# Indices and attention kept on chip, features three quads ahead, and the sort's turns copied by VectorE in a two-layer graph network

## The chip, the cores and the metric

The kernel runs on one core of one Trainium2 chip. The metric is the device time of one launch in microseconds (us), median of three runs. The engines are named as in the profile: PE is TensorE, DVE VectorE, ACT ScalarE, POOL GpSimd, SP SyncE; SPq and ACTq are the DMA queues that SP and ACT feed.

## What is computed

A network of two layers on a graph of 6250 nodes with 64 features each and 206,250 edges. The edges are the pairs of 100,000 drawn ones, both ways, and one loop for each node, sorted by dst. All is float32.

```
h = relu(layernorm(x));  row, col = src, dst
# layer 0: four heads
e   = concat(h[row], h[col])
a   = pos[col] * exp(lrelu(gate_w2 @ lrelu(gate_w1 @ e)))
x   = x + mean over heads of segment_sum(a / segment_sum(a)[row] * lrelu(msg_w2 @ lrelu(msg_w1 @ e)), row)
h = relu(layernorm(x))
# layer 1: feat = edge_attr (64 numbers an edge), attn = edge_weight
m   = (h[src] * sigmoid(feat @ prob_w.T) + (feat @ review_w.T) * sigmoid(feat @ score_w.T) * attn) * cj[src]
x   = x + segment_sum(m, dst) * ci
```

## The kernel before

The edges are padded to 404 blocks of 512 (128 partitions, T = 4 tiles); 403 of them (NBW) hold edges. Four blocks are a quad, 101 quads (NQ) in all. The kernel uses that dst is sorted: a block's edges end in a narrow window of nodes, whose rows are read with one plain transfer, while the rows of src are gathered by index. The program has these stages.

Setup (0 to about 320 us). Loads, the layernorm on DVE, then the loop over the 49 node tiles that writes the table of window rows: PE turns and projects a tile (L1999, L2008, L2009, L2019), ACT copies it (L1020, L1027, L1034), SP stores it. SP issues the setup's loads in the order of the program text; `loaded` counts 17 of them, from the first weights to the four of gate_w2 (L543), and ACT's L1037 waits for all.

Layer 0 (320 to 3640 us). Per block PE runs twelve matmuls of 512 columns (L1870, L1871) and many smaller ones; POOL gathers the rows of src from split_table (L774) with the indices in src_pairs, which SP loads two blocks at a time (load_index), after it has waited until the gathers that read the old ones are done. Sums are scattered to DRAM by POOL.

The node update between the layers takes to about 3704 us and ends in src_table, which holds a node's features and cj.

Layer 1 (3704 to 6366 us). Each engine has a program of its own in the order of the blocks b (m = b mod 4 is the place in the quad), tied to the others by semaphores.
- SP, load1_windows: at m = 0 it waits for `terms1_step` 16·(quad−1), which says that quad−2 is done and its buffers are free, then loads the quad's indices (src_quads, L592), features (512 KB, L594) and attention (attn_quads, L596), each in two buffers; then it waits for `out_ready` quad−1 and loads the x and ci windows (L624, L625).
- POOL, gather1_windows (L827): at m = 0 it waits for those three loads. In every block it waits for `terms1_step` 4·(b−3), that is until DVE is through with block b−4, whose gather buffer it fills (four buffers, ends1_windows), and issues four indirect gathers.
- DVE: two products of the features with the gates' weights (L1740), two reductions to dots (L1746); at m = 1 finish_rows for quad−2, which waits for PE's projection and writes the rows of the output (L1755); at m = 2 match_carry (L1761); the one-hot matrix (L1772); a part of the check; then feat_gate (L1777, waits for ACT's sigmoid), the terms (L1779, waits for the gather), L1782 and L1785. The last four step `terms1_step`, so L1785 is the end of a block on DVE.
- ACT: the sigmoid (L1132), copy_window (L1156) and send_rows (L1173, the store of the output rows) at m = 2, copy_turned (L1162, waits for PE's turn of the window) at the last m.
- PE: eight matmuls of a block (L2107) into ps_beta, at the quad's end the carry (L2112), the turn of the window (L2124), the projections (L2130, L2131).

The check runs beside layer 1: it sorts keys of the edges and compares them with the mirrored list; its result decides at the end whether the form with windows stands or a general form is run. sort_plan lays it on blocks from 10 to MIRROR = 380. HALVES are steps on DVE (L1644, L1647, up to 128x1024 elements), ROUNDS are turns: PE transposes four 128x128 pieces of a run into one PSUM bank (turn_bank, ps_hidden[2]), ACT copies the bank to the other list (L1116, or L1118 with a sign), two rounds in each of 28 blocks, so 56, and four more for the mirrored list (L1125). One bank serves all, so each turn waits for the copy before it. The columns and dot weights that DVE reads in every block (columns_ps, dots_w_ps) lie in another bank, ps_T.

## Time and profile before

| | us |
|---|---|
| median of 3 runs | 6369.76 |
| fastest, slowest | 6354.51, 6380.25 |
| the profiled execution, its own time | 6382.29 |
| its span | 6380.7 |
| PE, DVE, ACT, POOL busy | 4448.9, 4638.8, 2628.9, 3558.8 |
| setup, layer 0, update, layer 1 | 0 to 320, 320 to 3640, 3640 to 3704, 3704 to 6366 |

The span runs from the first to the last instruction of the profiled execution. An engine's busy time is the sum of its instructions without their waits. No engine is busy for more than 73% of the span, and the shares are means over stages with different limits, so the argument is made stage by stage. "<-issue" is idle time in which the engine waited for nothing that the profile shows; "<-remote" is a wait whose releaser the profile doesn't name.

### The profile page before, as it was taken

What the parts mean: (1) busy time and instruction counts of PE and PEld (TensorE: products, weight loads), DVE (VectorE), ACT (ScalarE), POOL (GpSimd) and SP (SyncE); (2) the same over time, 40 slices, a digit from 0 to 9 for tenths busy, and PEclk for the clock granted to TensorE, in tenths of its full rate; (3) what the DMA queues carried; (4) which work ended last, traced back from release to release, by engine and by line L of the source; (5) the groups of instructions that cost most, each with busy time, mean ns of one, the idle gap of its engine ahead of it and who ended that gap; (6) DMA issues with size and microseconds to landing.
All of it is one profiled execution on the core that took longest, in us unless ns stands there. A gap on an engine that the chain in (4) does not pass through costs nothing.

```text
span 6380.7 us, 112465 instructions
## 1 busy us (share of the span) xinstructions
PE 4448.9 (70%) x25026; PEld 2772.9 (43%) x25026; DVE 4638.8 (73%) x10169; ACT 2628.9 (41%) x6414; POOL 3558.8 (56%) x3640
## 2 busy tenths in 40 slices
PE   5799999999999999999999723333344443344443
PEld 4455555555555555555555323333333333333333
DVE  3488888888888888888888766666666666666664
ACT  3666667666666666666666510000000000000000
POOL 0255555555555555555555355656656556666664
PEclk8999999999999999999999855555555555555555
DMA  7533333333333333333333322222222222222222
GB/s 195 184 75 74 75 76 74 75 75 75 74 75 73 77 73 74 75 75 75 75 75 75 87 81 42 44 43 44 44 42 43 43 43 43 47 44 43 44 44 39
DMA packets 484894, 436.01 MB, mean 68 GB/s; under 512 B 294336, under 2 KB 366240, under 8 KB 483744
## 3 DMA queue, kind: packets, MB, share of 16 engines
q0 software_dynamic: 122512, 173.81, 15.7%
q1 hardware_dynamic: 334416, 247.54, 14.7%
q10 hardware_dynamic: 27840, 13.23, 1.1%
q8 instruction: 48, 0.79, 0.1%
q14 instruction: 78, 0.64, 0.0%
HBM read 363.28 MB, written 70.96 MB: 68 GB/s over the span
## 4 chain that ended last, share of the span: by engine, by line
PE 39%; issue 25%; DVE 10%; POOL 6%; SPq 6%; DMA 5%; ACT 4%; another core or an unknown queue 4%; DVEq 1%; ACTq 0%; POOLq 0%
PE ps_beta L1922 12%; PE ps_hidden L1870 8%; PE ps_hidden L1871 7%; POOL work L827 4%; DVE work L1358 3%; PE ps_sum L1941 3%; POOL ends L827 3%; PE ps_beta L1930 3%; PE ps_alpha L1904 1%; DMA attn_quads<-in_edge_weight 1%; SPq L592 1%; DMA ends<-src_table,src_quads 1%; PE ps_alpha L1913 1%; ACT beta_scaled L969 1%
## 5 line engine op out<-in xcount | busy, mean ns | idle before, releaser
L774 POOL DMA_INDIRECT ends<-split_table,src_pairs x1612 | 1578.0, 979 | 1615.7 <-issue 1459.6
L827 POOL DMA_INDIRECT work<-src_table,src_quads x808 | 806.8, 998 | 856.4 <-DMA attn_quads<-in_edge_weight 361.8
L1870 PE MATMUL ps_hidden<-ends_parts,w_high 128*128 128x512 f32 x2418 | 1097.4, 454 | 159.2 <-ACT ends_hot L964 60.0
L1358 DVE TENSOR_TENSOR work<-work,ps_hidden 128x512 f32<-128x512 f32 x1612 | 1101.0, 683 | 54.7 <-ACT work L911 43.5
L2107 PE MATMUL ps_beta<-work,equal 128*128 128x128 f32 x1616 | 411.4, 435 | 904.8 <-DVE work L1785 540.2
L911 ACT ACTIVATE work<-ps_hidden 128x512 f32<-128x512 f32 x1612 | 947.2, 600 | 219.3 <-PE ps_hidden L1871 179.6
L1871 PE MATMUL ps_hidden<-ends_hot,window 128*128 128x512 f32 x2418 | 954.5, 395 | 4.1 <-issue 3.8
L827 POOL DMA_INDIRECT ends<-src_table,src_quads x804 | 802.7, 998 | 257.9 <-issue 244.1
L1363 DVE TENSOR_TENSOR beta<-beta_scaled,ps_beta 128x512 f32<-128x512 f32 x806 | 551.4, 684 | 418.1 <-ACT beta_scaled L969 346.5
L1132 ACT ACTIVATE ps_alpha<-dots 128x8 f32<-128x8 f32 x403 | 72.4, 180 | 1876.9 <-DVE dots L1746 1336.8
L2107 PE MATMUL ps_beta<-work,dst_rows_sb 128*128 128x128 f32 x1608 | 411.4, 437 | 609.6 <-DVE work L1785 430.1
L1922 PE MATMUL ps_beta<-work,msg_w_sb 128*64 128x512 f32 x3224 | 827.6, 611 | 4.6 <-issue 0.9
L1870 PEld LDWEIGHTS ps_hidden<-ends_parts,w_high 128*128 128x128 f32 x2418 | 453.7, 188 | 793.3 <-DVE work L1358 436.0
L969 ACT ACTIVATE beta_scaled<-ps_beta 128x512 f32<-128x512 f32 x806 | 484.9, 602 | 701.8 <-PE ps_beta L1922 663.3
L2107 PEld LDWEIGHTS ps_beta<-work,equal 128*128 128x128 f32 x1616 | 354.5, 323 | 951.7 <-DVE work L1785 563.9
L2107 PEld LDWEIGHTS ps_beta<-work,dst_rows_sb 128*128 128x128 f32 x1608 | 355.2, 325 | 679.3 <-DVE work L1785 482.2
L1358 DVE TENSOR_TENSOR work<-scaled,ps_hidden 128x512 f32<-128x512 f32 x806 | 545.9, 677 | 25.7 <-ACT scaled L911 13.7
L911 ACT ACTIVATE scaled<-ps_hidden 128x512 f32<-128x512 f32 x806 | 486.0, 603 | 149.0 <-PE ps_hidden L1871 144.9
L1930 PE MATMUL ps_beta<-ident,beta 128*128 128x128 f32 x3224 | 506.1, 279 | 0.8 <-DVE beta L1363 0.7
L1871 PEld LDWEIGHTS ps_hidden<-ends_hot,window 128*128 128x128 f32 x2418 | 457.7, 189 | 44.3 <-issue 4.3
L1930 PEld LDWEIGHTS ps_beta<-ident,beta 128*128 128x128 f32 x3224 | 357.2, 141 | 167.6 <-issue 146.6
L788 POOL DMA_DIRECT2D sums<-key_rows x403 | 373.6, 927 | 75.1 <-issue 46.8
(202 smaller groups left out, 6703.2 us busy)
## 6 DMA issues: line engine op xcount, KB each, us to landing
window<-window_table SPq DMA_DIRECT2D x403, 192.5 KB
parts<-in_edge_attr SPq DMA_DIRECT2D x101, 512.0 KB
dst_rows_sb<-in_dst_rows SPq DMA_DIRECT2D x403, 128.0 KB
ends<-split_table,src_pairs POOLq DMA_INDIRECT x1612
window_table<-parts SPq DMA_DIRECT2D x49, 386.0 KB
sums<-key_rows POOLq DMA_DIRECT2D x403, 32.6 KB
work<-src_table,src_quads POOLq DMA_INDIRECT x808
ends<-src_table,src_quads POOLq DMA_INDIRECT x804
```

Of the source, the lines that this page charges most:

```text
L774: pool.indirect_dma_start(out=ends[m][:, t, :], out_offset=None, in_=split_table, in_offset=bass.IndirectOffsetOnAxis(ap=src_pairs[m // 2] ...
L788: pool.dma_start(sums0[0][bass.ds(first, WIN0), :], quad_sum[m * WIN0:(m + 1) * WIN0, :], accum_op=ALU.add).then_inc(quad_added, 16)
L827: pool.indirect_dma_start(out=ends1_windows[m][:, t, :], out_offset=None, in_=src_table, in_offset=bass.IndirectOffsetOnAxis(ap=src_quads[ ...
L911: nc.scalar.activation(scaled[k % NL][:, :], ps_hidden[k % NL][:, :], ACT.Copy, scale=SLOPE).then_inc(scaled_ready, 1)
L969: nc.scalar.activation(beta_scaled[:, a * B:(a + 1) * B], ps_beta[a][:, :], ACT.Copy, scale=SLOPE).then_inc(beta_scaled_ready, 1)
L1358: nc.vector.tensor_tensor(hidden[k][:, :], scaled[k % NL][:, :], ps_hidden[k % NL][:, :], ALU.max).then_inc(hidden_ready, 1)
L1363: nc.vector.tensor_tensor(beta_T[a], beta_scaled[:, a * B:(a + 1) * B], ps_beta[a][:, :], ALU.max).then_inc(beta_ready, 1)
L1870: nc.tensor.matmul(o, w1_high[:, k * P:(k + 1) * P], ends_parts[j][:, :], start=True, stop=False)
L1871: nc.tensor.matmul(o, window[j][:, k * P:(k + 1) * P], ends_hot[j][:, :], start=False, stop=True).then_inc(hidden_done, 1)
L1922: last = nc.tensor.matmul(ps_beta[a][i * D:(i + 1) * D, :], msg_w2_sb[:, 2 * a + i, :], hidden[2 + 2 * a + i][:, :], start=True, stop=True)
L1930: last = nc.tensor.transpose(ps_beta[a][:, t * P:(t + 1) * P], beta_T[a][:, t * P:(t + 1) * P], ident[:, :])
L2107: last = nc.tensor.matmul(ps_beta[odd][0:WIN, 0:W1], hot_four[m][:, t, :], terms1_windows[m][:, t, :], start=(m == 0 and t == 0), stop=(m ...
```

## The change

1. The indices (src) and attention of all blocks are kept on chip. In setup SP loads eight pieces of up to 128 block rows (128x512, 1.65 MB in all), four of each, ahead of the loads of gate_w2; DVE casts the indices to float at tile 11 of the loop over node tiles, PE turns each piece with four transposes (between tiles 14 and 33), DVE copies them to src_all and attn_all. POOL waits for the indices before its first gather, PE for both before layer 0. load_index, src_pairs, src_quads and attn_quads go, and with them POOL's waits on loads.
2. The features of layer 1 lie in four buffers instead of two. SP asks for quad+3 once quad−1 is done.
3. send_rows is issued by SP, between the load of the features and that of the x window, no longer by ACT.
4. PE turns the sort's pieces a block earlier and into two banks in turn (ps_hidden[2], ps_T), DVE copies them (move_rounds), in place of ACT. The mirrored list is added two pieces a block. columns_ps and dots_w_ps move from ps_T to ps_sum.
5. POOL's programs of both layers are written out block by block, where they were loops of hardware.

```diff
@@ SP, setup and layer 0
-            def load_index(b, a):
-                sp.dma_start(src_pairs[a][:, :].rearrange("p (b t) -> p b t", t=T),
-                             src[bass.ds(b, 2)].rearrange("b p t -> p b t")).then_inc(index_in[a], 16)
-            for a in range(2):
-                load_index(2 * a, a)
+            for k in range(4):
+                n = min(P, NB - k * P)
+                sp.dma_start(rows_sb[k][0:n, :].bitcast(I32),
+                             src_rows[k * P:k * P + n].rearrange("b t p -> b (t p)")).then_inc(rows_in[0], 16)
+            for k in range(4):
+                n = min(P, NB - k * P)
+                sp.dma_start(rows_sb[4 + k][0:n, :],
+                             edge_weight[k * P:k * P + n].rearrange("b p t -> b (p t)")).then_inc(rows_in[1], 16)
...
-                if m % 2 == 1 and not (isinstance(b, int) and b >= NB - 4):
-                    for n in (m - 1, m):
-                        sp.wait_ge(gathered0[n], 64 * (quad + 1))
-                        settle(sp)
-                    load_index(b + 3, m // 2)
@@ SP, layer 1
-            def load1_quad(quad, odd):
...
+            def load_feat(quad):
+                k = quad % 4
+                sp.dma_start(feat_quads[k].rearrange("p b t d -> p b (t d)"),
+                             edge_attr[bass.ds(4 * quad, 4)].rearrange("b p t d -> p b (t d)")).then_inc(feat_in[k], 16)
...
-            def load1_windows(b, quad, half, m, odd):
-                if m == 0 and not first_quads(quad):
-                    sp.wait_ge(terms1_step, 16 * (quad - 1))
-                    settle(sp)
-                    load1_quad(quad, odd)
-                    sp.wait_ge(out_ready, quad - 1)
-                    settle(sp)
-                if m == 0:
-                    load_x_window(quad, odd)
...
-            quads(sp, load1_windows)
+            sp.wait_ge(part_free, NCH)
+            load_feat(3)
+            for quad in range(NQ):
+                if quad >= 1 and quad + 3 < NQ:
+                    sp.wait_ge(terms1_step, 16 * quad)
+                    load_feat(quad + 3)
+                if quad >= 2:
+                    send_rows(quad - 2)
+                load_x_window(quad)
@@ POOL
-                pool.wait_ge(index_in[m // 2], 16 * (quad + 1))
...
-                        in_offset=bass.IndirectOffsetOnAxis(ap=src_pairs[m // 2][:, m % 2 * T + t:m % 2 * T + t + 1],
+                        in_offset=bass.IndirectOffsetOnAxis(ap=src_all[:, b * T + t:b * T + t + 1],
...
+            pool.wait_ge(src_ready, 4)
...
-            fours(pool, edges0_windows)
+            for b in range(NBW):
+                edges0_windows(b, b // 4, b % 4)
...
-                if m == 0:
-                    pool.wait_ge(edge_in1w[odd], 48 * (half + 1))
                 if not first_four(b):
                     pool.wait_ge(terms1_step, 4 * (b - 3))
...
-                        in_offset=bass.IndirectOffsetOnAxis(ap=src_quads[odd][:, m, t:t + 1], axis=0)).then_inc(gathered1w[m], 16)
+                        in_offset=bass.IndirectOffsetOnAxis(ap=src_all[:, b * T + t:b * T + t + 1], axis=0)).then_inc(gathered1w[m], 16)
...
-            quads(pool, edges1_windows)
+            every_block(edges1_windows)
@@ ACT, layer 1
-                if b in ROUNDS:
-                    move_rounds(*ROUNDS[b])
-                if b - MIRROR in (0, 1):
-                    mirror_rounds(2 * (b - MIRROR))
-                if m == 2 and not (isinstance(quad, int) and quad < 2):
-                    send_rows(quad - 2, odd)
@@ DVE
+            def cast_rows():
+
+                dve.wait_ge(rows_in[0], 64)
+                for k in range(4):
+                    n = min(P, NB - k * P)
+                    nc.vector.tensor_copy(rows_sb[k][0:n, :], rows_sb[k][0:n, :].bitcast(I32)).then_inc(rows_cast, 1)
+
+            def keep_rows(a, k):
+
+                dve.wait_ge(rows_turned, 4 * a + k + 1)
+                n = min(P, NB - k * P)
+                kept = (src_all, attn_all)[a].rearrange("p (b t) -> p t b", t=T)[:, :, k * P:k * P + n]
+                nc.vector.tensor_copy(kept, row_banks[k % 2][:, :].rearrange("p (t b) -> p t b", b=P)[:, :, 0:n]).then_inc(src_ready, 1)
...
+            def move_rounds(n, first, of, turned_by):
+
+                for i in range(first, first + 2):
+                    dve.wait_ge(sort_turned, 4 * n + i + 1)
+                    if turned_by is None:
+                        nc.vector.tensor_copy(runs[1 - of][:, i * B:(i + 1) * B], turn_banks[i % 2][:, :]).then_inc(sort_moved, 1)
+                    else:
+                        nc.vector.tensor_scalar(runs[1 - of][:, i * B:(i + 1) * B], turn_banks[i % 2][:, :],
+                                                signs[:, turned_by:turned_by + 1], None, ALU.mult).then_inc(sort_moved, 1)
...
                 if m == 0:
-                    dve.wait_ge(edge_in1w[odd], 48 * (half + 1))
+                    dve.wait_ge(feat_in[quad % 4], 16 * (quad // 4 + 1))
@@ PE
+            def turn_rows(a, k):
...
+                for c in range(T):
+                    rows = (rows_sb[k][0:n, c * P:(c + 1) * P] if a == 0 else
+                            rows_sb[4 + k][0:n, :].rearrange("b (p t) -> b t p", t=T)[:, c, :])
+                    last = nc.tensor.transpose(row_banks[k % 2][:, c * P:c * P + n], rows, ident[0:n, 0:n])
+                last.then_inc(rows_turned, 1)
...
+            pe.wait_ge(src_ready, 8)
...
-                wait(pe, sort_moved, 4 * n + i)
+                wait(pe, sort_moved, 4 * n + i - 1)
                 for c in range(4):
-                    last = nc.tensor.transpose(turn_bank[:, c * P:(c + 1) * P],
+                    last = nc.tensor.transpose(turn_banks[i % 2][:, c * P:(c + 1) * P],
                                                runs[of][:, (4 * i + c) * P:(4 * i + c + 1) * P], ident[:, :])
```

## Rows read from the trace of the kernel before

**Rows 1.** Windows by stage: start:end, length, busy of each engine, PEclk, DMA, GB/s.
```profile
36.00:235.00 199.00, 133.56 (x684) 98.52 (x682) 22.65 (x78) 91.19 (x245) 11.52 (x12) 0.87 0.87 252
320.00:3640.00 3320.00, 3166.62 (x19672) 1728.50 (x19670) 2808.14 (x5510) 2275.68 (x5209) 1895.74 (x1961) 1.00 0.35 74
3704.00:6366.00 2662.00, 1059.92 (x4166) 895.80 (x4166) 1660.45 (x4330) 160.49 (x661) 1609.48 (x1612) 0.51 0.23 45
```

**Rows 2.** Lines of POOL in layer 1: busy, mean ns of one, idle before and releasers.
```profile
L827 POOL DMA_INDIRECT work<-src_table,src_quads x808 | 806.8, 998 | 856.4 <-DMA attn_quads<-in_edge_weight 361.8 <-issue 241.3 <-DVE work L1785 110.2
L827 POOL DMA_INDIRECT ends<-src_table,src_quads x804 | 802.7, 998 | 257.9 <-issue 244.1 <-DVE work L1785 13.5 <-DVE ps_sum L1782 0.3
```

**Rows 3.** Windows of three runs of gathers with the pause behind each.
```profile
3704.00:3767.00 63.00, 13.23 (x51) 11.46 (x52) 24.89 (x65) 1.36 (x7) 37.93 (x41) 0.50 0.34 97
4907.50:4962.00 54.50, 19.44 (x75) 16.68 (x76) 31.67 (x81) 1.98 (x11) 33.04 (x32) 0.50 0.22 42
5409.70:5436.30 26.60, 13.44 (x52) 11.52 (x53) 17.93 (x46) 1.27 (x6) 16.01 (x16) 0.50 0.23 43
```

**Rows 4.** Timeline of the second run's end: start, length, instruction, idle before it.
```profile
4935.03 0.69 PE L2131 MATMUL ps_hidden<-window_sum,ident 128*128 128x64 f32 x2
...
4949.05 0.94 POOL L827 DMA_INDIRECT ends<-src_table,src_quads  x1 [0.30 <-issue]
4953.21 0.28 DVE L1755 SCALAR_TENSOR_TENSOR parts<-ps_hidden,ci_windows,parts 128x64 f32<-128x64 f32 x1 [14.36 <-remote]
...
4955.86 0.42 DVE L1785 TENSOR_TENSOR work<-parts,ps_sum 128x256 f32<-128x256 f32 x1
4955.89 0.38 SPq L592 DMA_DIRECT2D src_quads<-in_src  x1
...
4962.15 0.94 POOL L827 DMA_INDIRECT work<-src_table,src_quads  x1 [12.15 <-DMA attn_quads<-in_edge_weight]
```

**Rows 5.** Waits named "remote": us in total, times, longest.
```profile
ACT parts L1162 <- remote: 238.3, 57, 19.8
...
DVE parts L1755 <- remote: 158.6, 18, 14.5
```

**Rows 6.** Setup: timeline of SPq, ACT, DVE and PE, and PE's line L1930.
```profile
8.75 1.51 SPq L535 DMA_DIRECT2D src_pairs<-in_src  x2
...
22.14 0.83 ACT L1037 ACTIVATE near_parts<-w_near 128x768 fp32r<-128x768 f32 x1
...
33.22 0.20 DVE L1247 COPY table_sb<-pos_sb 128x49 f32<-128x49 f32 x1
...
151.72 0.19 PEld L2008 LDWEIGHTS ps_beta<-near_parts,h_T 128*128 128x128 f32 x1 [0.65 <-ACT h_T L1020]
...
L1930 PE MATMUL ps_beta<-ident,beta 128*128 128x128 f32 x3224 | 506.1, 279 | 0.8 <-DVE beta L1363 0.7
```

**Rows 7.** Lines: POOL's gathers in layer 0.
```profile
L774 POOL DMA_INDIRECT ends<-split_table,src_pairs x1612 | 1578.0, 979 | 1615.7 <-issue 1459.6
```

**Rows 8.** Lines of DVE in layer 1: the mirrored list's addition out of a bank.
```profile
L1694 DVE TENSOR_TENSOR x_sb<-ps_hidden,table_sb 128x512 f32<-128x512 f32 x4 | 2.8, 692 | 18.6 <-PE ps_hidden L2069 9.7 <-remote 7.8 <-issue 1.1
```

**Rows 9.** Timeline: gathers beside DVE's L1740 and beside L1647.
```profile
5004.89 0.74 DVE L1740 TENSOR_TENSOR work<-parts,ps_T 128x256 f32<-128x256 f32 x2
...
5005.28 0.94 POOL L827 DMA_INDIRECT ends<-src_table,src_quads  x1 [0.30 <-issue]
...
5014.41 1.22 DVE L1647 TENSOR_TENSOR centered<-table_sb 128x1024 f32<-128x1024 f32 x1
5014.59 1.86 POOL L827 DMA_INDIRECT work<-src_table,src_quads  x1 [0.31 <-issue]
```

**Rows 10.** Timeline: the end of the first run of gathers.
```profile
3752.82 0.94 POOL L827 DMA_INDIRECT work<-src_table,src_quads  x1 [0.30 <-issue]
...
3759.62 0.35 DVE L1761 TENSOR_SCALAR parts<-ps_T,carry_at 128x128 f32<-128x128 f32 x1 [7.33 <-remote]
...
3766.95 0.94 POOL L827 DMA_INDIRECT ends<-src_table,src_quads  x1 [13.19 <-DVE work L1785]
```

More of the change, by code:

```diff
@@ L133, in gnn @@
         ones = sb("ones", [1, P])
-        w1_near = sb("w1_near", [P, HID])
+        first_rows = sb("first_rows", [P, NB * T])
+        w1_near, w1_far = [first_rows[:, a * HID:(a + 1) * HID] for a in range(2)]
+        attn_all = first_rows[:, :]
         columns = sb("columns", [P, WIN])
@@ L328, in gnn @@
         window_copied = sem("window_copied")
-        edge_in1w = [sem(f"edge_in1w{j}") for j in range(2)]
+        feat_in = [sem(f"feat_in{k}") for k in range(4)]
+        rows_in = [sem(f"rows_in{a}") for a in range(2)]
+        rows_cast = sem("rows_cast")
+        rows_turned = sem("rows_turned")
+        src_ready = sem("src_ready")
         gathered1w = [sem(f"gathered1w{m}") for m in range(4)]
@@ L352, in gnn @@
         begun_again = sem("begun_again")
-        index_in = [sem(f"index_in{a}") for a in range(2)]
         gathered0 = [sem(f"gathered0_{m}") for m in range(4)]
@@ L477, in sort_plan @@
         def sort_plan():
-            halves, rounds, of, steps, moved, turn, b = {}, {}, 0, 1, 0, 0, SORT_FROM
+            halves, rounds, moves, of, steps, moved, turn, b = {}, {}, {}, 0, 1, 0, 0, SORT_FROM
             def kept(run):
@@ L494, in sort_plan @@
                     for r in range(2):
-                        rounds[b + r] = (turn, 2 * r, of, None if inward or k == SORT_BITS else k - RUN_BITS, steps)
+                        rounds[b - 1 + r] = (turn, 2 * r, of, steps)
+                        moves[b + r] = (turn, 2 * r, of, None if inward or k == SORT_BITS else k - RUN_BITS)
                     of, turn, moved, b = 1 - of, turn + 1, 4 * turn + 4, b + 2
@@ L499, in sort_plan @@
                         of, steps, b = two_halves(1 << i, run, inward and i == k - RUN_BITS - 1, RUN)
-            return halves, rounds, of, steps, turn, b
-        HALVES, ROUNDS, SORTED, SORT_STEPS, TURNS, MIRROR = sort_plan()
-        SETTLE = MIRROR + 6
+            return halves, rounds, moves, of, steps, turn, b
+        HALVES, ROUNDS, MOVES, SORTED, SORT_STEPS, TURNS, MIRROR = sort_plan()
+        SETTLE = MIRROR + 5
         assert SETTLE + 9 < NBW
@@ L603, in _ @@
             for quad in range(2):
-                load1_quad(quad, quad)
+                load_feat(quad)
             sp.wait_ge(sums0_landed, 1)
@@ L626, in load_x_window, with send_rows @@
                              ).then_inc(x_window_in[odd], 16)
+            def send_rows(quad):
+                first = window_start(sp, 4 * quad)
+                sp.wait_ge(out_ready, quad + 1)
+                if quad == 0:
+                    sp.wait_ge(out_set, 16)
+                else:
+                    sp.wait_ge(rows_out, 16 * quad)
+                settle(sp)
+                sp.dma_start(out[bass.ds(first, WIN), :], out_rows[quad % 2]).then_inc(rows_out, 16)
             sp.wait_ge(x_summed, 2 * NCH)
@@ L1162, in copy_turned @@
                 nc.scalar.activation(sum_T, sum_turned, ACT.Copy).then_inc(sum_T_ready, 1)
-            def send_rows(quad, odd):
-                first = window_start(act, 4 * quad)
-                act.wait_ge(out_ready, quad + 1)
-                if isinstance(quad, int) and quad == 0:
-                    act.wait_ge(out_set, 16)
-                else:
-                    act.wait_ge(rows_out, 16 * quad)
-                settle(act)
-                act.dma_start(out[bass.ds(first, WIN), :], out_rows[odd]).then_inc(rows_out, 16)
             copy_constants()
             every_block(edges1_windows)
-            send_rows(NQ - 2, (NQ - 2) % 2)
             copy_window(NQ - 1, (NQ - 1) % 2)
             copy_turned(NQ - 1)
-            send_rows(NQ - 1, (NQ - 1) % 2)
             fit = fits(act)
@@ L1517, in _ @@
                     signs_of_lanes()
+                elif t == 11:
+                    cast_rows()
+                elif 18 <= t < 38 and t % 6 < 2:
+                    keep_rows((t - 18) // 12, 2 * ((t - 18) // 6 % 2) + t % 6)
             dve.wait_ge(fits_step, 9)
@@ L1713, in settle_part @@
                     dve.wait_ge(reach_turned, 1)
-                    nc.vector.tensor_reduce(out=reach[0:1, 7:8], in_=turn_bank[0:1, 0:P], axis=AX.X,
+                    nc.vector.tensor_reduce(out=reach[0:1, 7:8], in_=turn_banks[0][0:1, 0:P], axis=AX.X,
                                             op=ALU.max).then_inc(mirror_step, 1)
```

127 lines of the change are left out of this document (67 added, 60 removed).

## The prediction

> **What bounds the kernel now.** I read the windows by stage first, then the lines and waits of POOL in the second layer, then the windows of single runs of gathers, then the timeline inside one of them, then the waits put down to "remote".
>
> By stage [rows 1]: the first layer's main loop (320 to 3640 us) has PE busy 3166.62 of 3320 us. PE is its bound, and at 95% busy it leaves nothing to an edit that touches only loads. The second layer (3704 to 6366) lasts 2662 us and no engine fills it: POOL 1609, DVE 1660, PE 1060, ACT 160. It handles 403 blocks of 512 edges, 2662 / 403 = 6.606 us each, and issues 1612 indirect gathers, four to a block.
>
> POOL is the engine to follow there [rows 2]. One gather takes 0.998 us and is followed by some 0.30 us of issue time (244.1 / 804): 1.30 us, so 5.19 us a block and 2093 us for all. The other 569 us of the stage are pauses of POOL. The rows put 361.8 us of them down to the DMA of the quad's attention and indices and 110.2 to DVE's L1785, which is the wait for a free gather buffer. DVE needs 1660 / 403 = 4.12 us a block, less than POOL's 5.19. So POOL would be the bound were it not stopped.
>
> The stops have a period [rows 3]. From 4907.5 to 4962.0 POOL does 32 gathers (8 blocks) and then pauses: 54.5 us, 6.81 a block. From 5409.7 to 5436.3 it does 16 gathers in 26.6 us, 6.65 a block. The first run, from 3704 to 3767, has 40 gathers (its 41st row is the next run's) in 63 us. The view says "DMA", but the timeline [rows 4] shows what lies behind the DMA. PE's last matmul of the quad, L2131, ends at 4935.72. DVE wants its result (L1755) and starts only at 4953.21, after 14.36 us "remote", with no unfinished matmul in front of it. All that time POOL issues gathers, to 4949.99. DVE is released 3.2 us after POOL's last gather and finishes its block (L1785 ends 4956.28); SP then issues the held index load (L592 at 4955.89), and POOL goes on at 4962.15, 12.15 us after it stopped. So the loop is a circle: while POOL issues gathers without a pause, PE's completion signals reach DVE and ACT late; DVE stops; POOL runs on until it has no work left; the signal lands; the load and then POOL start again. The waits named "remote" [rows 5] are this: ACT L1162 238.3 us, DVE L1755 158.6 us (18 times, longest 14.5). Only what comes after DVE's release is the DMA.
>
> **The change part by part.**
> Setup. Eight row loads are added to SP's queue ahead of the loads of gate_w2, two index loads are taken out. At the 0.76 us of one of those two (1.51 / 2) [rows 6] the queue grows by 6 × 0.76 = 4.5 us. Everything that ACT's L1037 waits for has landed by 22.14 now; with 4.5 us and the 1.65 MB of the rows at the 252 GB/s of [rows 1] (6.5 us) it lands by 33.1, and DVE wants L1037's result after L1247, at 33.4: hidden, at worst 0.5 us late. The 32 transposes (8 × 4) cost 0.28 us each by L1930, 9.0 us, in a loop of 49 steps, each of which has PE wait for ACT's h_T (its weight load at 151.72 after 0.65 us). Bounds 0 (they fit in the 65 us that PE is idle from 36 to 235) and +15 (9.0 plus a semaphore turn of 0.7, an estimate from that 0.65, for each of eight). I take +5. DVE's 4 casts and 8 copies lie in 176 us of idle DVE.
> First layer. 202 small index loads, SP's waits on finished gathers and POOL's waits on the loads go. POOL's gathers of this stage show 1615.7 us of idle time before them [rows 7], and the bound is PE: 0, bounds −10 and +5 (POOL's loop is unrolled, whose instruction fetch this trace does not show).
> Second layer, indices and features. POOL no longer waits for a load, so SP's late index load can't stop it, and features are there two quads earlier. What is late next is the free buffer. DVE stopped in block b (L1755 is in the second block of a quad) lets POOL gather up to block b+3, where now it stops with the quad, at b+2: a run of 32 gathers becomes one of 36. Its length: the run that began at 4907.5 ended at 4949.99, 42.5 us for 32, 1.33 each, so 36 × 1.33 = 47.8 us. Its pause: 3.2 us from the last gather to the late signal, 3.1 us until DVE ends that block (4953.21 to 4956.28), 0.7 us to POOL's start (estimate, a semaphore turn as above): 7.0 us instead of 12.15. The cycle is 54.8 us for 9 blocks, 6.09 a block. Were the stop to come 25 us after the start of a run (in [rows 4] it is 31), 11 us of run-ahead and 7.0 us of pause give 43.3 us for 29 gathers, 5.97 a block. The first run of all, whose indices were there from the start, took 6.30. I take 6.05, the middle of the first two moved a little towards the third: 403 × 6.05 = 2438 us, −224. The waits at L1785 (110.2 us now) become the rule and are no term of their own. Bounds of the part: −569 (no pauses) and +70 (the slower rival).
> Sort turns. 60 copies of 128x512 out of a bank move from ACT to DVE. DVE's own operation on such a bank, L1694, takes 0.692 us [rows 8]: 60 × 0.69 = 41 us, 0.10 a block, against a slack of 5.19 − 4.12 = 1.07. POOL's pace hides it; with DVE on the path it would be +41: bounds 0 and +41. PE turns a block earlier, so DVE seldom waits for a timely turn. A late one now stops DVE itself in 30 blocks, where before it stopped ACT and DVE behind it: 0, bounds −40 and +40.
> What DVE's copies do to POOL. The gather beside DVE's L1647, which has two inputs in SBUF, lasts 1.86 us; the one beside L1740, whose second input is a bank, 0.94 [rows 9]. The copies have one input, a bank, and so cost POOL nothing; if they acted as L1647 it would be 60 × 0.92 = +55 us. The Trainium skill ("SBUF — State Buffer", section "Who interferes with whom") says that a DVE instruction with at most one SBUF input outside the 2-port modes does not contend with GpSimd and that one with two contends with its reads. The trace agrees on both, and by the rule, too, the term is 0.
> Output rows. send_rows leaves ACT's queue for SP's. The wait it makes (the rows of quad−2, finished in the second block of the quad) stood in SP's queue already, ahead of load_x_window, and the features are asked for before it. Behind it is only the x window, which is read two quads later. 0.
> Sum on the profiled execution (6382.29 us, span 6380.7): −224 + 5 = −219, 6163. That execution lies 12.5 us above the median of the three timed runs (6369.76), so against the median I say 6150.
>
> **The rivals.**
> A: the late signals come from something that goes with the index waits, and POOL keeps its pace. The second layer takes 403 × 5.19 = 2093 us: 6382 − 569 + 5 − 12 = 5806. For it: DVE has 1.07 us a block to spare, and four buffers. Against it: in [rows 4] DVE waits for PE, not for an index, and the first run stopped as well, after 40 gathers. The Trainium skill, in the same section, says "PE and ACT never wait on anyone"; by that rule nothing that POOL does could hold PE's results back, and this rival alone would be left. The trace disagrees: 14.36 us between a finished matmul and its reader. Half-way cases (rarer or shorter stops) give 5880 to 6040.
> B, slower: the release takes longer the longer POOL has run, because more signals stand in line. After 32 gathers it came 3.2 us behind the last one. In the first run [rows 10] the last of 40 gathers ended at 3753.76, DVE was released at 3759.62, 5.9 us later, and POOL's pause was 13.19 us with no DMA in it. With 36 gathers in 47.8 us the cycle is even with now at 9 × 6.606 − 47.8 = 11.7 us of pause; beyond it the change loses. With 13.2: 61.0 / 9 = 6.78 us a block, 2732, +70: 6382 + 70 + 5 − 12 = 6445. For it: that pause. Against it: that run was longer, and its gathers took 1.25 us each, so that even with it a block took 6.30.
> C, no change: DVE's stops follow the number of signals it needs from PE, not POOL's runs, and what a pause loses in length it gains in number: 6340 to 6400. For it: runs of 16 and of 32 gathers come to 6.65 and 6.81 a block, near each other. Against it: in both, some 6 us from DVE's release to POOL's first gather are the load's, and go.
>
> **How the numbers follow.** The forecast has 0.50, with a range of its own of 6040 to 6260 (5.8 to 6.33 us a block); A 0.20; between A and the forecast 0.10; C 0.10; B 0.10. The range is 5800 to 6320: it takes in A and the bounds of the unknown costs above the forecast (+15, +41, +55 and +40, not all at once) and leaves out B and C. Faster by over 0.5%: 0.50 + 0.20 + 0.10 = 0.80; within 0.5% (about what can be told from no change here): 0.10; slower: 0.10.
>
> **What would show it.** POOL's waits on a load of indices are gone, its pauses are released by DVE's last operation of a block and last about 7 us, after runs of some 36 gathers (12 us or more: B; runs of hundreds: A). "Remote" waits stay at DVE's finish_rows and ACT's copy_turned. The second layer lasts about 2440 us, the first layer's loop stays within 10 us, setup grows by 5. DVE's copies out of the banks take 0.6 to 0.7 us, with gathers of 0.94 beside them. The prediction is wrong if the signals come in time without a pause of POOL, or if the stops move into the first layer.

## The result and the profile after

| | us |
|---|---|
| before, median of 4 runs | 6369.69 (6354.51 to 6380.25) |
| changed, median of 4 runs | 6123.82 (6118.99 to 6131.07) |
| ratio, 95% interval | 0.9603 (0.9581 to 0.9626) |
| profiled executions, before and changed | 6382.29 and 6118.99 |
| forecast, range | 6150, 5800 to 6320 |

The changed kernel is 4.0% faster. Between the two profiled executions the time by stages, taken from the first product of layer 0 to the first one of its last block and from the first to the last gather of layer 1, is:

| stage | before | changed | difference | forecast |
|---|---|---|---|---|
| setup, to the first product | 235.9 | 230.8 | −5.1 | +5 |
| layer 0, to the last block's product | 3388.9 | 3315.4 | −73.5 | 0 |
| update, to the first gather of layer 1 | 79.2 | 80.4 | +1.2 | 0 |
| layer 1, to the last gather's start | 2660.1 | 2469.2 | −190.9 | −224 |
| the end | 16.6 | 20.5 | +3.9 | 0 |

The windows of the changed kernel, in the columns of [rows 1]: setup's loop, layer 0, layer 1.

```profile
36.00:230.80 194.80, 132.13 (x716) 98.73 (x715) 30.66 (x91) 90.61 (x245) 11.56 (x12) 0.91 0.87 258
230.80:3546.20 3315.40, 3217.47 (x20102) 1774.82 (x20103) 2871.58 (x5630) 2341.52 (x5333) 1932.97 (x1998) 1.00 0.34 76
3626.60:6096.70 2470.10, 1049.57 (x4154) 890.52 (x4155) 1671.29 (x4377) 114.59 (x598) 1618.44 (x1612) 0.52 0.23 47
```

Layer 1 takes 2470 / 403 = 6.13 us a block; 6.05 was forecast, 6.61 it was. ACT's busy time fell from 160 to 115 us, and the pace is still set by no engine's busy time: POOL has 1618 of 2470 us. Its lines, which answer to [rows 2], and its waits (total, times, longest):

```profile
L839 POOL DMA_INDIRECT ends<-src_table,parts x804 | 813.0, 1011 | 313.4 <-issue 240.6 <-DVE work L1800 72.8
L839 POOL DMA_INDIRECT work<-src_table,parts x808 | 805.5, 997 | 601.0 <-DVE work L1800 308.4 <-issue 229.9 <-DMA src_table<-table_sb 62.8
```
```profile
POOL work L839 <- DVE work L1800: 308.4, 124, 7.5
POOL ends L839 <- DVE work L1800: 72.8, 44, 10.4
```

The DMA of the indices is gone from them. L1800 is the old L1785, the end of DVE's block: POOL now pauses only for a free buffer, 381 us in all, where it lost 361.8 to the load and some 124 to that. The waits for PE's signals did not go, they grew; the rows answer to [rows 5], L1150 being the old L1162 and L1770 the old L1755:

```profile
ACT parts L1150 <- remote: 432.5, 39, 19.7
DVE parts L1770 <- remote: 379.1, 55, 15.3
...
ACT ps_alpha L1126 <- remote: 56.4, 7, 12.4
...
DVE ps_sum L1797 <- remote: 52.2, 15, 5.2
```

The last two rows are not about PE: L1126 is ACT's sigmoid, which waits for DVE's dots, and L1797 (the old L1782) waits only for DVE's own operations in front of it. So what is late is not PE's signals alone.

Counted in both traces (gaps of more than 2 us between gathers), POOL's pauses went from 87 of 6.66 us on the mean to 77 of 4.75 us, 579 to 366 us. A timeline of the changed kernel, to be held against [rows 4], shows one stop with its parts:

```profile
4771.97 0.42 PE L2160 MATMUL ps_hidden<-ident,window_sum 128*64 128x128 f32 x1
...
4783.59 0.95 POOL L839 DMA_INDIRECT ends<-src_table,parts  x1 [0.31 <-issue]
4786.96 0.27 ACT L1150 ACTIVATE parts<-ps_hidden 64x128 f32<-64x128 f32 x1 [15.38 <-remote]
...
4788.06 0.42 DVE L1800 TENSOR_TENSOR work<-parts,ps_sum 128x256 f32<-128x256 f32 x1
...
4789.26 0.95 POOL L839 DMA_INDIRECT work<-src_table,parts  x1 [4.72 <-DVE work L1800]
```

PE turned the window by 4772.39; ACT, which waits for it, starts at 4786.96, 2.4 us after POOL's last gather of this run of 32 ended (4784.54). ACT's sigmoid stands behind that copy, DVE behind the sigmoid, and POOL behind DVE's L1800: 2.4 + 1.5 to the end of L1800 + 0.8 = 4.7 us. It is the circle of the forecast without its load.

But not every late signal waits for such a pause. Layer 1 has 130 waits named remote of over 2 us, 109 of them for PE (the others for DVE). Of the 109, 64 end in a pause of POOL (a gap of over 1 us) and 45 in the midst of its gathers; in the kernel before these were 71 and 19 of 91. One of DVE's for PE ended 45 us after POOL's last pause:

```profile
4662.69 0.95 POOL L839 DMA_INDIRECT work<-src_table,parts  x1 [0.31 <-issue]
4663.68 0.28 DVE L1770 SCALAR_TENSOR_TENSOR parts<-ps_hidden,ci_windows,parts 128x64 f32<-128x64 f32 x1 [10.79 <-remote]
...
4663.94 0.95 POOL L839 DMA_INDIRECT work<-src_table,parts  x1 [0.30 <-issue]
```

### The profile page after: what moved, and what is told of

It reads as the page before. It is cut to its first block, busy times and chain, and to the rows that moved or that the text cites. A ratio compares the mean times of both kernels' runs of the same rounds, so it can differ in the third digit from the quotient of the medians.

```text
span 6116.3 us, 108132 instructions
## 1 busy us (share of the span) xinstructions
PE 4418.4 (72%) x25058; PEld 2776.0 (45%) x25058; DVE 4662.3 (76%) x10241; ACT 2592.6 (42%) x6354; POOL 3568.6 (58%) x3639
## 4 chain that ended last, share of the span: by engine, by line
PE 38%; DVE 32%; issue 12%; another core or an unknown queue 12%; ACT 3%; DMA 1%; DVEq 1%; ACTq 0%; POOL 0%; SPq 0%; POOLq 0%
PE ps_beta L1937 11%; PE ps_hidden L1885 8%; PE ps_hidden L1886 6%; DVE dots L1761 4%; DVE work L1333 4%; PE ps_beta L1945 3%; PE ps_sum L1956 3%; DVE table_sb L1640 3%; DVE work L1755 3%; DVE centered L1640 3%; DVE work L1794 2%; DVE work L1800 2%; PE ps_alpha L1919 2%; DVE equal L1787 2%
## 5 line engine op out<-in xcount | busy, mean ns | idle before, releaser
L786 POOL DMA_INDIRECT ends<-split_table,parts x1612 | 1581.0, 981 | 1532.9 <-issue 1399.2
L839 POOL DMA_INDIRECT work<-src_table,parts x808 | 805.5, 997 | 601.0 <-DVE work L1800 308.4
L839 POOL DMA_INDIRECT ends<-src_table,parts x804 | 813.0, 1011 | 313.4 <-issue 240.6
L1126 ACT ACTIVATE ps_alpha<-dots 128x8 f32<-128x8 f32 x403 | 72.0, 179 | 1841.8 <-DVE dots L1761 1156.8
```

The source lines that it names most:

```text
L786: pool.indirect_dma_start(out=ends[m][:, t, :], out_offset=None, in_=split_table, in_offset=bass.IndirectOffsetOnAxis(ap=src_all[:, b * T ...
L839: pool.indirect_dma_start(out=ends1_windows[m][:, t, :], out_offset=None, in_=src_table, in_offset=bass.IndirectOffsetOnAxis(ap=src_all[:, ...
```

## The experiments

Each number of a stage below is read as in the table above, and each ratio is to the kernel before of the same session, with its 95% interval. The runs fell into four sessions, and the kernel before, run in each beside the others, took 6370.87, 5618.80, 6307.43 and 5621.26 us in them. That is itself the main finding, and it comes with the second session. (The expectations call the sessions chips; what the runs show is only that the same kernel took another time.)

**POOL's loops written out, nothing else** (before 6370.87).

```diff
-            fours(pool, edges0_windows)
+            for b in range(NBW):
+                edges0_windows(b, b // 4, b % 4)
...
-            quads(pool, edges1_windows)
+            every_block(edges1_windows)
```

> The kernel before, with POOL's programs of both layers written out block by block; nothing else. Layer 0 became 73 us shorter with the change (3389 us from the first product to the last before, 3315 after), where I had counted nothing. Theory U (POOL's loop of hardware delays its gathers or what waits for them): this run shows layer 0 at about 3320 us and the whole some 70 us shorter than before. Theory L (the small index loads on SP's queue, their packets and SP's waits on gathers cost it): layer 0 stays at 3389 within 8 us. In layer 1 both expect 2660 us within 20, since the loads and POOL's wait for them are still there.

Measured: 6379.76 us, ratio 1.001 (0.9991 to 1.0029). Layer 0 3381.8, layer 1 2672.1 us. Of the 73.5 us of layer 0 the loops have at most the 7 that it is shorter here, and nothing of layer 1's gain; theory U falls.

**Layer 0's small index loads put back** (before 6370.87).

```diff
+                if m % 2 == 1 and not (isinstance(b, int) and b >= NB - 4):
+                    for n in (m - 1, m):
+                        sp.wait_ge(gathered0[n], 64 * (quad + 1))
+                        settle(sp)
+                    sp.wait_ge(index_in[m // 2], 16 * quad)
+                    settle(sp)
+                    load_index(b + 3, m // 2)
```

> The changed kernel with layer 0's 202 small index loads put back on SP's queue, with SP's waits for the gathers before them, into tiles that nobody reads and with nobody waiting for them. Theory L expects layer 0 back at about 3389 us (+73) and the whole near 6197. Theory U expects no change: layer 0 at 3315 within 8, the whole 6124 within 15. A part of it would say that POOL's wait for the load, which this run lacks, had the rest. Layer 1 stays at 2469 within 20 in both.

Measured: 6209.89 us, ratio 0.9728 (0.9702 to 0.9754), 86 us above the changed kernel. Layer 0 3393.2 us (+77.8), layer 1 2478.3. Theory L holds, and without an engine that waits for these loads (SP alone asks that the one of a quad earlier has landed): 200 loads (the first two are not repeated) of 256 pieces of 16 bytes, with SP's waits, cost layer 0 its 78 us. PE, the bound, idles 143 us of layer 0 here, 98 in the changed kernel and 148 in the one before; the other 33 of the 78 us are longer busy time of the same matmuls, which no row explains. In the idle time the wait for ACT's copy ends_hot moves (before, changed, this run):

```profile
PE ps_hidden L1870 <- ACT ends_hot L964: 60.0, 94, 1.0
```
```profile
PE ps_hidden L1885 <- ACT ends_hot L976: 9.2, 40, 0.6
```
```profile
PE ps_hidden L1898 <- ACT ends_hot L989: 44.2, 81, 0.9
```

ACT, in its turn, is held at the copies of PE's product; its line over the same 1600 us (1000 to 2600) of the changed kernel and of this one:

```profile
L923 ACT ACTIVATE work<-ps_hidden 128x512 f32<-128x512 f32 x778 | 461.3, 601 | 61.0 <-PE ps_hidden L1886 41.0 <-issue 10.5
```
```profile
L936 ACT ACTIVATE work<-ps_hidden 128x512 f32<-128x512 f32 x759 | 446.7, 600 | 84.4 <-PE ps_hidden L1899 66.8 <-issue 11.9
```

There are four such copies a block: 194.5 blocks in the first, 189.75 in the second. The copies themselves are the same (0.60 us); ACT waits 26 us longer for PE. In all of layer 0 ACT, idle, began such a copy over 1 us after PE's matmul had ended 35 times in the changed kernel, 78 times here and 89 times in the kernel before; so lateness of PE's signals is here too, in small pieces.

**Features as late as before, POOL waits for them** (before 6370.87).

```diff
-                if quad >= 1 and quad + 3 < NQ:
-                    sp.wait_ge(terms1_step, 16 * quad)
-                    load_feat(quad + 3)
+                if quad >= 4:
+                    sp.wait_ge(terms1_step, 16 * (quad - 1))
+                    load_feat(quad)
...
+                if m == 0:
+                    pool.wait_ge(feat_in[quad % 4], 16 * (quad // 4 + 1))
```

> The changed kernel with the features asked for as late as before (quad q once quad q-2 is done) and POOL waiting for them at each quad's first block, as it did for the indices. My forecast's account (the circle of late signals, DVE's stop, and a load that POOL waits for) expects layer 1 to go back from 2469 to about 2640 us (+150 to +190) with POOL's pauses released by a DMA, 5 to 12 us long, and the whole near 6290. Rival: the gain of layer 1 came from somewhere else (the 292 small packets a quad of indices and attention that are gone, code written out, copies on DVE), then layer 1 stays within 30 us of 2469.

Measured: 6332.90 us, ratio 0.9937 (0.9911 to 0.9963), 209 us above the changed kernel; layer 1 2687.8 us (+218.6), layer 0 3310.2. POOL's wait for a load costs what the forecast's account says and more: 29 us more than the upper end of the expectation, with 59 pauses of 10.2 us on the mean. The rival falls. One pause in the timeline of this kernel, with SP's load in it (L596) and POOL 4.7 us behind it; the 10.88 us are 3.7 to the late signal, 2.6 to the load and 4.7 of the load, though the row names an operation of DVE:

```profile
4627.57 0.94 POOL L841 DMA_INDIRECT ends<-src_table,parts  x1 [0.30 <-issue]
4632.17 0.28 DVE L1772 SCALAR_TENSOR_TENSOR parts<-ps_hidden,ci_windows,parts 128x64 f32<-128x64 f32 x1 [2.92 <-remote]
...
4634.73 0.42 SPq L596 DMA_DIRECT2D parts<-in_edge_attr  x1
4639.39 0.94 POOL L841 DMA_INDIRECT work<-src_table,parts  x1 [10.88 <-DVE ps_sum L1799]
```

**finish_rows two blocks later** (before 6370.87).

```diff
-                if m == 1 and not (isinstance(quad, int) and quad < 2):
-                    finish_rows(quad - 2, half - 1, odd)
...
+                if m == last_m(quad) and quad >= 2:
+                    finish_rows(quad - 2, half - 1, odd)
```

> The changed kernel with finish_rows (DVE's wait for PE's projection) moved from the second block of a quad to its last, after the one-hot matrix. Late signals have DVE stop there 55 times for 379 us in the changed kernel, the longest 15.3 us. If DVE stops because it asks for PE's result only about a block and a half after PE was due, two more blocks (12 us) take most of these stops away: DVE's waits there fall below 100 us, the cycle lengthens and layer 1 goes from 2469 towards 2300 us, by 60 to 170 us. Rival: the lateness is held by POOL's run of gathers, not by the time that has passed, so the signal comes only when POOL pauses; then another wait for PE (the window's copy or the one-hot's buffers, four blocks back) stops DVE or ACT a block or two later, POOL's runs become longer by as much as DVE's stop comes later, and layer 1 changes by less than 60 us.

Measured: 6082.40 us, ratio 0.9534 (0.9513 to 0.9554); layer 1 2434.0 us (−35), with 62 pauses instead of 77, of 4.91 us each. It beats both kernels, 41 us under the changed one. But the rival's account is what happened: DVE no longer waits at finish_rows, and DVE and ACT wait elsewhere instead, for PE (L1144, L1150, L1785) and for DVE's own signals (L1126, L1797), and POOL's runs are longer (median 24 gathers for 20). The rival's premise, that a signal comes only when POOL pauses, fits 56 of this run's 91 waits for PE of over 2 us; 35 end in the midst of gathers.

```profile
ACT parts L1150 <- remote: 599.6, 41, 26.0
ACT ps_alpha L1126 <- remote: 118.8, 14, 12.4
DVE ps_sum L1797 <- remote: 118.4, 28, 6.3
ACT window_sum L1144 <- remote: 81.7, 19, 9.5
DVE equal L1785 <- remote: 75.7, 12, 15.1
```

**Three gathers of four left out** (before 5618.80).

```diff
-                for t in range(T):
+                for t in range(1):
...
-                dve.wait_ge(gathered1w[m], 64 * (quad + 1))
+                dve.wait_ge(gathered1w[m], 16 * (quad + 1))
```

> The changed kernel with one indirect gather a block in layer 1 instead of four: three quarters of the rows of src are left out of it, all else is the same. If PE's completion signals are late because POOL issues gathers without a pause, they are timely here: the waits called remote (812 us at ACT's L1150 and DVE's L1770 in the changed kernel) all but go, below 60 us, and layer 1 runs at DVE's own pace, 4.15 us a block and a few tenths for the waits between engines: 1700 to 1900 us. Rival: PE's signals are late for a reason of PE's or of DVE's (its fp32 matmuls, the chain of window, turn and projection): then the remote waits stay above 300 us and layer 1 above 2000 us.

Measured: 5212.18 us, one run; layer 1 1685.8 us, 4.18 a block, and no wait named remote. Both numbers are as the theory expected, but they can't decide it: beside it, with before at 5618.80, the kernels with all gathers have no remote waits either. What it shows is DVE's pace, 4.18 us a block.

**POOL paced by PE's signals**, twice (before 5618.80 and 5621.26).

```diff
                     pool.wait_ge(terms1_step, 4 * (b - 3))
+                    pool.wait_ge(summed1_done, b - 3)
```

> The changed kernel with one more wait of POOL in layer 1: before the gathers of block b it waits until PE's signal of block b-4 is there. POOL then stops of itself as soon as a signal is about a block late, where now it runs on until DVE's stop has used up the four buffers. The late-signals theory (the signals land 2 to 3 us after a gather, if no other follows) expects more and shorter pauses of POOL, about 3 us each after 12 to 16 gathers, DVE's and ACT's remote waits cut to less than half of 812 us, and layer 1 between 2350 and 2470 us (16 gathers in 20.8 us and 3 us of pause are 5.95 us a block, 2398 us). Rival: the pause costs as much as it saves; the sum of pauses is set by how many signals have to land, and layer 1 stays at 2469 within 30, or grows when POOL waits for PE at every block (to 2600).

> The changed kernel with one more wait of POOL in layer 1: before the gathers of block b until PE's signal of block b-4 is there. On a chip where PE's signals come late the theory (they land 2 to 3 us after a gather if no other follows) expects more and shorter pauses of POOL, DVE's and ACT's remote waits less than half of the changed kernel's, and layer 1 shorter than its 2469 us by 20 to 100. Rival: the sum of the pauses is set by the signals that have to land; layer 1 within 30 us of 2469, or up to 2600 when POOL waits for PE at every block. On a chip where they come in time it repeats 5641 in all, with no wait of POOL for PE over 1 us.

Measured: 5641.38 us, ratio 1.0037 (1.0026 to 1.0049), and 5642.59 us, ratio 1.0040 (1.0026 to 1.0054). Layer 1 2125.2 and 2119.4 us, layer 0 3196.1 and 3195.9. Neither expectation was tested, since no signal was late for the new wait to catch; the idea stays open. The second expectation's last sentence held.

**Features late, POOL waits for no load**, twice (before 5618.80 and 6307.43). The first edit of the run with POOL's wait, without its second.

> The changed kernel with the features asked for as late as before (quad q once quad q-2 is done), but with POOL waiting for no load; only DVE waits for the features. With POOL's wait layer 1 took 2688 us, without both it takes 2469. If POOL's wait for the load is what closes the circle, layer 1 stays within 40 us of 2469 here. If the features' early start is what counts (DVE waits for them at a quad's start, then runs late), layer 1 comes to 2600 or more, with DVE's L1755 waiting for the features. I give the first two in three: after a pause POOL goes on at once.

> The changed kernel with the features asked for as late as before, POOL waiting for no load. On a chip where PE's signals come late: if POOL's wait for the load closes the circle, layer 1 stays within 40 us of 2469, where with POOL's wait it took 2688; if the features' early start counts, it comes to 2600 or more, with DVE's L1755 waiting for the features. On a chip where they come in time it repeats 2094 us of layer 1, 5612 in all.

Measured, with before at 5618.80: 5612.44 us, ratio 0.9987 (0.9977 to 0.9996), layer 1 2094.0. With before at 6307.43: 6065.77 us, ratio 0.9625 (0.9603 to 0.9648), layer 1 2437.1, beside 2436.7 of the changed kernel beside it. So the wait of POOL for a load is what closes the circle; that the features are asked for three quads ahead brings nothing. (The run with POOL's wait, 2687.8 us, is of the first session; the 250 us between it and this one are far more than the 32 us between the sessions' changed kernels.)

**Index loads of whole rows**, twice (before 5618.80 and 5621.26).

```diff
-                sp.dma_start(src_pairs[a][:, :].rearrange("p (b t) -> p b t", t=T),
-                             src[bass.ds(b, 2)].rearrange("b p t -> p b t")).then_inc(index_in[a], 16)
+                sp.dma_start(src_pairs[:, :],
+                             src_rows[bass.ds(b, 2)].rearrange("b t p -> (b t) p")).then_inc(index_in[a], 16)
...
-                    sp.wait_ge(index_in[m // 2], 16 * quad)
+                    sp.wait_ge(index_in[1 - m // 2], 16 * (quad + m // 2))
```

The edit is against the run with the small loads. All loads go to one tile, so SP here waits for the load just before, not for that of a quad earlier.

> The changed kernel with the 202 index loads of layer 0 and SP's waits before them, as in the run that took layer 0 from 3315 to 3393 us, but each load reads the same 4 KB as eight whole rows of 512 bytes instead of 256 pieces of 16 bytes. If the small packets do the harm (they hold up what carries PE's signals to ACT and DVE), layer 0 is back at 3315 within 10. If it is SP's waits (the next window's loads issued late behind them) or the load as such, layer 0 stays near 3393.

> The changed kernel with the 202 index loads of layer 0 and SP's waits before them, each load reading the same 4 KB as eight whole rows of 512 bytes instead of 256 pieces of 16 bytes. With the small pieces layer 0 went from 3315 to 3393 us on a chip where PE's signals come late. On such a chip: if the small packets do the harm, layer 0 is within 12 us of the changed kernel's, and the ratio to the kernel before is that of the changed kernel, 0.96; if SP's waits or the load as such do it, layer 0 is 60 us or more longer and the ratio 0.975. On a chip where they come in time it says nothing: layer 0 3196 us, 5643 in all.

Measured: 5642.66 us, ratio 1.0038 (1.0025 to 1.0050), and 5642.77 us, ratio 1.0044 (1.0027 to 1.0060); layer 0 3196.1 and 3196.2 us. As for the packets, this says nothing, for the same reason. But layer 1 of this kernel is that of the changed kernel, and its windows (layers 0 and 1; the run beside 5621.26) show what that one would do where PE's signals are in time:

```profile
225.00:3421.20 3196.20, 3146.54 (x20102) 1789.93 (x20103) 2873.51 (x5630) 2332.94 (x5333) 1936.96 (x1998) 1.00 0.36 79
3500.40:5627.00 2126.60, 1062.67 (x4166) 899.89 (x4166) 1697.52 (x4390) 118.31 (x601) 1635.63 (x1612) 0.51 0.26 55
```

The engines' busy times are those of the changed kernel above within 4%, and so is the granted clock (1.00 and 0.51). POOL issues its 1612 gathers of layer 1 without one gap above 0.32 us. The timeline of a quad's end, to be held against [rows 4], with L2182, L1785 and L1815 for the old L2131, L1755 and L1785:

```profile
4752.58 0.69 PE L2182 MATMUL ps_hidden<-window_sum,ident 128*128 128x64 f32 x2
...
4755.62 0.94 POOL L854 DMA_INDIRECT work<-src_table,parts  x1 [0.30 <-DVE work L1815]
...
4756.60 0.28 DVE L1785 SCALAR_TENSOR_TENSOR parts<-ps_hidden,ci_windows,parts 128x64 f32<-128x64 f32 x1
...
4756.87 0.94 POOL L854 DMA_INDIRECT work<-src_table,parts  x1 [0.30 <-issue]
```

DVE takes PE's result in its turn, without a wait, in the midst of gathers. In layer 0 ACT's copies into work, over 1000 to 2600 us, have 201.5 blocks and hardly a wait for PE; none of them in all of layer 0, idle before, began more than 0.12 us after PE's matmul:

```profile
L938 ACT ACTIVATE work<-ps_hidden 128x512 f32<-128x512 f32 x806 | 481.0, 604 | 25.9 <-issue 8.6 <-PE ps_hidden L1901 4.0
```

The line's other copies (into scaled) wait longer for PE than before, 125 us against 57 in the changed kernel, since ACT comes to them early. What counts is the idle time of PE, the bound: 50 us in all of layer 0, against 98.

**The changed kernel again** (before 6307.43).

> The changed kernel once more, to be read beside the kernel before on the same chip. The last four runs were on a chip on which the kernel before takes 5619 us, not 6370, and no wait for PE is named remote there: POOL issues all 1612 gathers of layer 1 without one pause, 2095 to 2126 us. On such a chip the change has nothing to gain: layer 1 at 2120 us and layer 0 at 3196 as in the two variants that share them, the whole at 5610 to 5645, within 0.5% of the kernel before. On a chip like the first one (before 6370) it repeats 6124 within 15 us. The rival, that the chip is only faster all round, expects the change to keep its 4% on either chip.

Measured: 6066.44 us, ratio 0.9630 (0.9601 to 0.9658): layer 0 3288.7, layer 1 2436.7 us, remote waits at L1150 483 and at L1770 323 us. A session that the expectation doesn't name, 57 us quicker than 6124, with the gain kept (3.7%). Whether it is lost where signals are in time was not run for the changed kernel itself. The two variants nearest to it, the one paced by PE, whose added wait shows nothing above 0.32 us, and the one with whole-row loads, say that it is: 0.4% slower than the kernel before; the one with the features late is 0.1% faster.

## Why the prediction was right, and where it was not

The time was 26 us under the forecast, 6124 for 6150. One half of the forecast's mechanism is shown: PE's signals stay late, the load drops out of the circle, the free buffer takes its place (the waits at L1800; 219 us come back with POOL's wait). The other half, that the signals are late because POOL issues gathers without a pause, and land when it stops, is not. It fits 64 of the 109 waits for PE of over 2 us; 45 end in the midst of gathers, DVE's own signals are late too (L1797), and in the quicker sessions POOL never pauses and no signal is late. So POOL's run of gathers can't be the whole cause, and what it has to do with it stays open. That the total came so near is luck in part: layer 1 gave 33 us less than forecast, layer 0 gave 73.5 that weren't in the sum. By its own steps:

- Setup, +5: it was −5.1. The transposes and copies lie under the loop's waits; POOL's first gather is 50 us later (134.9 for 84.9), which nothing waits for. The lower bound was the better value; the 5 us themselves are hardly beyond what kernels with one setup differ by where before takes 6370 (230.2 to 232.9 us to the first product with the new one, 234.0 and 235.9 with the old).
- Layer 0, 0 with bounds −10 and +5: it was −73.5. This is the step that failed. I read "PE 95% busy" as "nothing to gain from loads". But the 148 us in which PE idled (98 now, 50 where signals are in time) held waits for ACT's copies, which in turn began late after PE's own matmuls, and with the loads and SP's waits back both grew again: +77.8 us in all, 45 of them idle time of PE and 33 its longer busy time.
- Layer 1, −224: it was −190.9, 6.13 us a block for 6.05. The sum is near and its terms are not: runs of 36 gathers with pauses of 7.0 us were forecast, the median run has 20 (16 with the gaps over 1 us) and the mean pause 4.75 us. The signal that lands in a pause is as often for ACT, at copy_turned (26 of the 77), as for DVE at finish_rows (25), where it was 47 and 12 of 87; for ACT's only 1.5 us of DVE's block, not 3.1, are left after it. Both terms are too large, so that their quotient is nearly right, which is luck: 7.0 / 9 = 0.78 us of pause a block forecast, 366 / 403 = 0.91 measured. The forecast's second cycle has a slip besides: its 29 gathers in 36 us are 1.25 us each, where the first cycle takes 1.33; with 1.33 they are 27, the cycle is 6.4 us a block in place of 5.97, and the middle of the two 6.2 in place of 6.05. The measured 6.13 lies between.
- Copies on DVE, 0: right. They take 0.68 us (L1688) and 0.74 with a sign (L1690), and the 42 gathers that overlap one of the 56 take 0.946 us on the mean, 0.948 at most, as the rows and the rule of the Trainium skill ("SBUF — State Buffer", "Who interferes with whom") had it. The timeline shows two. All of POOL's gathers of layer 1 are stretched by 96 us in all, as against 89 before (what each takes above 0.945 us, added up).

```profile
4524.50 0.94 POOL L839 DMA_INDIRECT work<-src_table,parts  x1 [0.30 <-issue]
4524.56 0.68 DVE L1688 COPY table_sb<-ps_hidden 128x512 f32<-128x512 f32 x1
4525.15 0.68 DVE L1688 COPY table_sb<-ps_T 128x512 f32<-128x512 f32 x1
...
4525.75 0.95 POOL L839 DMA_INDIRECT work<-src_table,parts  x1 [0.30 <-issue]
```

- Output rows, 0: nothing in the trace speaks against it.
- Rival A named 2093 us for a layer 1 without late signals, with a chance of 0.20. It is false for the result. For the sessions in which before takes 5620 us its number fits, 2094 with the features late, 2119 to 2126 with them early, since POOL keeps its pace there; its reason doesn't, for the kernel before, with its index waits, is as quick there. The Trainium skill's sentence "PE and ACT never wait on anyone" ("SBUF — State Buffer", "Who interferes with whom") is on the engines' SBUF ports. The prediction stretched it to the time at which others see PE's results; the 14.36 us are a wait of DVE's, so that they don't contradict the sentence, and no run here tests it.
- Rival B, a release that takes longer after longer runs, is right in its direction and fell by its size: in the changed kernel the release came 2.5 us after the last gather of runs of 13 to 20 (median) and 3.0 us after runs of 31 to 48, at most 3.7; the longest wait for L1800 is 10.4 us.
- Rival C expected more pauses for shorter ones; they became fewer, 77 for 87 (counted from 1 us, 91 in both).

What stays open: why signals are late in some sessions and not in others (the record gives the first two, 6371 and 5619 us, the same chip number, so that it may not be the chip), and what POOL's gathers have to do with it (no variant with fewer gathers, or with POOL held for PE's signals, ran where they are late); whether the small packets or SP's waits before them do the harm in layer 0; and whether a POOL that stops by itself helps.

## What to carry to other kernels

Look, for each engine that idles, at whether the instruction it waits for had ended long before ("remote" with nothing unfinished in front): that time is neither the busy engine's nor the load's. An edit far away can move a stage: 200 small loads that no engine waits for, with the waits in front of them on their own queue, made layer 0 78 us longer. A wait for a transfer that is issued only when a late consumer is done multiplies such lateness; take the transfer out of the loop (219 us here); asking for it earlier, with nobody but DVE waiting, brought nothing here. And run the kernel before beside every variant: a gain that comes from lateness may be there only where the lateness is, as the variants here suggest.

## What the runs showed of the hardware

- The same kernel took 6371, 6307, 5619 and 5621 us in four sessions, with its own runs within 0.4% of the median in each and the granted clock of the stages unchanged. In the quicker ones no trace has a remote wait of ACT or DVE for PE. The kernel before was 752 us, 12%, shorter there than in the first; no trace of it was taken in them, so that these 752 us are the late signals is drawn from variants of the changed kernel.
- Where signals are late, a wait of DVE's or ACT's for PE lasts up to 20 us with no unfinished matmul in front of it; in the changed kernel 64 of the 109 over 2 us end in a pause of POOL and 45 while it goes on issuing gathers. DVE waits for its own signals as well there, up to 5.2 us at L1797.
- Where signals are late, 200 transfers of 256 pieces of 16 bytes, in 3300 us, with SP's waits for gathers in front of them, made layer 0 2.3% longer, though no engine waits for the data. In the quicker sessions loads of the same bytes in whole rows, with the same kind of waits, cost nothing (3196 us with and without).
- Where they are in time, the kernel with the features' later start had a layer 1 25 to 32 us shorter than the two variants with the early one (2094 us against 2119 to 2126): the gathers into ends took 1.010 us on the mean instead of 1.040 to 1.049. Why they do, no run here shows.
